# Turning and spilling the first batch's expert gates inside wavelet attention, and reading them back behind two experts' weights

## The reference

```python
logits = xt @ wg                                  # 128 channels -> 8 experts
topv, topi = jax.lax.top_k(logits, top_k)         # top_k = 2
w = jax.nn.softmax(topv, axis=-1)
gates = (jax.nn.one_hot(topi, E, dtype=x.dtype) * w[..., None]).sum(axis=1)
y = jnp.zeros_like(xt)
for e in range(E):                                # E = 8, hidden width 512
    h = jax.nn.gelu(xt @ w1[e] + b1[e])
    y = y + gates[:, e:e + 1] * (h @ w2[e] + b2[e])
```

## Time and profile before

| | us |
|---|---|
| median of 3 runs | 4427.36 |
| lowest and highest | 4424.29, 4433.59 |
| the profiled execution | 4442.52 |
| its span in the trace | 4441.2 |

### The profile page before, as it was taken

One profiled execution on the slowest core, in us unless ns is written; L12 is line 12 of the kernel. 1 busy time (PEld: TensorE's weight loads), 2 busy tenths in 40 slices (PEclk: granted clock), 3 DMA queues, 4 the chain that ended last, 5 costly groups with the idle time before them and its releaser, 6 DMA issues.

```text
span 4441.2 us, 73631 instructions
## 1 busy us (share of the span) xinstructions
PE 3571.8 (80%) x28566; PEld 1826.3 (41%) x28566; DVE 3318.2 (75%) x5155; ACT 2848.1 (64%) x4792; POOL 970.4 (22%) x1447
## 2 busy tenths in 40 slices
PE   6999868999799998999996555555555558899998
PEld 4666512222344445676673111111111115566666
DVE  6777767786311127887886999999999996778887
ACT  3655415556234445666665999999998995566665
POOL 2444432100467640000001222222221210000000
PEclk8999859999899999999997555555555559999999
DMA  1000031231412100000001101111101110000000
GB/s 48 1 1 1 1 72 32 55 57 20 108 28 38 38 17 9 12 7 12 2 2 22 22 15 22 22 22 22 21 16 22 22 19 20 7 11 7 7 2 21
DMA packets 256809, 97.45 MB, mean 22 GB/s; under 512 B 223795, under 2 KB 241854, under 8 KB 256446
## 3 DMA queue, kind: packets, MB, share of 16 engines
q1 hardware_dynamic: 256462, 92.74, 10.5%
HBM read 31.75 MB, written 2.23 MB: 8 GB/s over the span
## 4 chain that ended last, share of the span: by engine, by line
PE 43%; DVE 27%; issue 14%; ACT 3%; DMA 1%; SPq 0%; POOL 0%; DVEq 0%; POOLq 0%; ACTq 0%
DVE d_negmax L2802 12%; PE psum L2333 7%; PE psum L2362 6%; DVE f_m_E L2432 6%; PE psum L2348 6%; PE psum L2029 5%; PE psum L2052 5%; PE psum L1420 3%; DVE wl_negmax L1538 2%; PE psum L1409 2%; DVE f_pT_E L2451 2%; PE psum L1397 2%; ACT d_junk L2860 2%; PE psum L2735 1%; PE psum L2724 1%
## 5 line engine op out<-in xcount | busy, mean ns | idle before, releaser
L2802 DVE TENSOR_REDUCE d_negmax<-psum 128x1 f32<-128x1024 f32 x1024 | 1176.0, 1212 | 52.2 <-PE psum L2735 51.1
L2860 ACT ACTIVATE d_junk<-psum,d_negmax 128x1024 bf16<-128x1024 f32 x1024 | 1138.9, 1114 | 103.8 <-DVE d_negmax L2802 96.1
L2735 PE MATMUL psum<-d_qT,d_kT 64*128 64x512 bf16 x2048 | 607.1, 602 | 547.7 <-ACT d_junk L2860 527.1
L2526 ACT ACTIVATE hidden<-psum,f_nm_E 128x1024 f32<-128x1024 f32 x512 | 566.5, 1113 | 146.8 <-DVE f_nm_E L2435 146.7
L2432 DVE TENSOR_REDUCE f_m_E<-psum 128x1 f32<-128x1024 f32 x512 | 602.0, 1217 | 48.4 <-PE psum L2333 47.2
L2735 PEld LDWEIGHTS psum<-d_qT,d_kT 64*128 64x128 bf16 x2048 | 105.8, 101 | 1050.4 <-ACT d_junk L2860 990.0
L2333 PE MATMUL psum<-f_k_E,f_q_swapped_E 64*128 64x512 f32 x1024 | 526.3, 624 | 6.6 <-ACT hidden L2526 6.6
L2333 PE MATMUL psum<-f_k_E,f_q_E 64*128 64x512 f32 x1024 | 526.0, 623 | 2.9 <-DVE f_v_E L2423 1.9
L2362 PE MATMUL psum<-f_pT_E,f_v_E 128*64 128x128 f32 x8192 | 505.4, 276 | 2.5 <-DVE residual L2462 2.5
L2533 ACT COPY f_pT_E<-psum 128x512 f32<-128x512 f32 x512 | 299.9, 586 | 318.8 <-PE psum L2348 318.8
L2451 DVE COPY f_pT_E<-psum 128x512 f32<-128x512 f32 x512 | 351.5, 686 | 162.7 <-PE psum L2348 153.2
(11 more groups left out here) (330 smaller groups left out, 4542.8 us busy)
## 6 DMA issues: line engine op xcount, KB each, us to landing
moe_gates_on_all<-moe_gate_spill SPq DMA_DIRECT2D x16, 1024.0 KB, 13.7
f_q_swapped_E<-f_q_E SPq DMA_DIRECT2D x64, 128.0 KB, 2.3
moe_w<-in_moe_w SPq DMA_DIRECT2D x15, 256.0 KB, 5.6
out<-residual SPq DMA_DIRECT2D x1, 2048.0 KB, 8.7
residual<-in_hidden_states SPq DMA_DIRECT2D x2, 768.0 KB, 8.3
wl_qT<-wl_q_rows SPq DMA_TRANSPOSE x48, 3.3
residual<-in_hidden_states SPq DMA_DIRECT2D x2, 256.0 KB, 3.2
m_taps<-in_m_conv SPq DMA_DIRECT2D x4, 128.0 KB
```

The costliest lines, as they stand in the source:

```text
L2526: A.activation(pb[:, u % 2, f * 2 * BANK:(f + 1) * 2 * BANK], two(2 * f), ACT.Exp, bias=nm[:, u % 4:u % 4 + 1], scale=SC, accum_out=rs[:, ...
L2735: last = T.matmul(bank(2 + 2 * (at % 3) + jj), kT[half, s, jb * P:(jb + 1) * P], qT[half, s, hf * BANK:(hf + 1) * BANK], start=True, stop= ...
L2802: V.tensor_reduce(mh[:, t % 2, n // 2, n % 2:n % 2 + 1], two(2 + 2 * (at % 3)), X, ALU.max, negate=True).then_inc(*maxed.up(at))
L2860: A.activation(junk[:, at % 3, :], two(2 + 2 * (at % 3)), ACT.Exp, bias=mh[:, t % 2, n // 2, n % 2:n % 2 + 1], accum_out=sh[:, t % 2, n // ...
```

## The change

The first batch's transposition, copy and spill leave the head of phase D and become a step `dgt` in phase C's list, after unit 29 of the last round. It takes a slot of PSUM in the rotation. SP, which had no step left in phase C by then, issues the spill there. In phase D the reads of batch 0's gates (`moe_gates_8` and both halves of `gall`) go ahead of the weights of experts 2 to 7, behind those of experts 0 and 1. For batch 1 nothing moves. The list `late` loses its first entry, so the two banks swap parts.

```diff
+            def pe_gates(b, bk):
+                T.wait_ge(*fd.gated(b))
+                T.transpose(bank(bk)[:, 0:P], fd.gcol[:, :, :].rearrange("p e i -> p (e i)"), ident[:, :]).then_inc(*fd.g_turned.up(b))
+            def dve_rows(b, bk):
+                V.wait_ge(*fd.g_turned(b))
+                if b:
+                    V.wait_ge(fd.spilled.sem, 16 * b)
+                V.tensor_copy(fd.grow[:, :], bank(bk)[:, 0:P]).then_inc(*fd.g_copied.up(b))
+            def sp_rows(b):
+                SP.wait_ge(*fd.g_copied(b))
+                SP.dma_start(fd.spill[b].rearrange("e (i p) -> (e i) p", p=P), fd.grow[:, :]).then_inc(*fd.spilled.one())
...
-                                  25: [("dgate", 5), ("dgate", 6)], 26: [("dgate", 7)], 27: [("dgate", 8)]},
+                                  25: [("dgate", 5), ("dgate", 6)], 26: [("dgate", 7)], 27: [("dgate", 8)], 29: [("dgt",)]},
...
-                paired = [s for s in seq if s[0] in ("turn", "qkv", "max", "exp", "norm", "co", "wo", "yt", "dch", "dlg")]
+                paired = [s for s in seq if s[0] in ("turn", "qkv", "max", "exp", "norm", "co", "wo", "yt", "dch", "dlg", "dgt")]
...
+                        elif kind == "dgt":
+                            fd.sp_rows(0)
...
-                late = [("gt", 0)]
+                late = []
...
+                def sp_gates(k):
+                    b, g = groups[k]
+                    if g == 0:
+                        if b:
+                            fd.sp_rows(b)
+                        SP.wait_ge(*spilled.all())
+                        SP.dma_start(g8[:, b, :], spill[b]).then_inc(*few.one())
+                    if k >= 2:
+                        SP.wait_ge(*scaled((k - 1) * E_ - 1, FT - 1))
+                    for half in range(2):
+                        es = slice(half * E_ // 2, (half + 1) * E_ // 2)
+                        SP.dma_start(gall[:, k % 2, es], wide(spill[b:b + 1, es, g * BANK:(g + 1) * BANK], 0, P)).then_inc(*spread[k % 2][half].one())
...
                         SP.dma_start(w2[:, e * FT:(e + 1) * FT, :], a["moe_w2"][e].rearrange("(f p) d -> p f d", p=P)).then_inc(*ldw[e].one())
-                    for k, (b, g) in enumerate(groups):
-                        if g == 0:
-                            SP.wait_ge(*g_copied(b))
-                            SP.dma_start(spill[b].rearrange("e (i p) -> (e i) p", p=P), grow[:, :]).then_inc(*spilled.one())
-                            SP.wait_ge(*spilled.all())
-                            SP.dma_start(g8[:, b, :], spill[b]).then_inc(*few.one())
...
+                        if e == 1:
+                            sp_gates(0)
+                    for k in range(1, NGR):
+                        sp_gates(k)
...
                 def pe():
                     enter(T)
-                    pe_gates(0)
...
                 def dve():
                     enter(V)
-                    dve_rows(0)
```

More of the change, by code:

```diff
@@ L1096, in front_D @@
             mx = sb(st, "moe_max", [P, NT])
+            fd.grow = sb(st, "moe_gate_rows", [P, P])
+            fd.spill = nc.dram_tensor("moe_gate_spill", (NB, E_, S), F32).ap()
+            fd.spilled = loads("moe_gates_spilled")
+            fd.g_copied = signal("moe_gate_rows_done", range(NB))
             fd.ld = loads("moe_first_loads")
@@ L1160, in dve_gates @@
                 yield
-            fd.sp_first, fd.pe_logits, fd.act_gates, fd.dve_gates = sp_first, pe_logits, act_gates, dve_gates
+            fd.sp_first, fd.sp_rows, fd.pe_logits, fd.pe_gates = sp_first, sp_rows, pe_logits, pe_gates
+            fd.act_gates, fd.dve_gates, fd.dve_rows = act_gates, dve_gates, dve_rows
             return fd
@@ L1354, in pe_slot @@
                             T.wait_ge(*fd.lg_read(0))
+                        elif kind == "dgt":
+                            T.wait_ge(*fd.g_copied(0))
                         elif kind == "co":
@@ L1481, in pe @@
                             fd.pe_logits(0, pe_slot("dlg"))
+                        elif kind == "dgt":
+                            fd.pe_gates(0, pe_slot("dgt"))
                     leave(T)
@@ L1654, in dve @@
                             next(gates, None)
+                        elif kind == "dgt":
+                            fd.dve_rows(0, slot("dgt"))
                     leave(V)
@@ L1896, in phase_D @@
             GE = NG4 * E_
-            gated, g_turned, b1 = fd.gated, fd.g_turned, fd.b1
+            gated, g_turned, g_copied, b1, spill, spilled = fd.gated, fd.g_turned, fd.g_copied, fd.b1, fd.spill, fd.spilled
             fr = front_E("E", fd.stack)
@@ L1903, in phase_D @@
                 b2 = sb(st, "moe_b2", [E_, D])
-                grow = sb(st, "moe_gate_rows", [P, P])
                 gall = sb(st, "moe_gates_on_all", [P, 2, E_, BANK])
@@ L1910, in phase_D @@
                 yT = sb(st, "moe_yT", [P, 2, BANK])
-                spill = nc.dram_tensor("moe_gate_spill", (NB, E_, S), F32).ap()
                 ld, ldw = loads("phase_loads"), [loads(f"moe_expert_loads_{e}") for e in range(E_)]
-                spilled = loads("moe_gates_spilled")
                 again = loads("token_loads")
@@ L1927, in phase_D @@
                 added = signal("moe_added", range(NGR))
-                g_copied = signal("moe_gate_rows_done", range(NB))
                 FIRST_CH, AT_LG, AT_GT = 12, 16, 25
@@ L2005, in pe_route @@
                         yield
-                    pe_gates(b)
+                    fd.pe_gates(b, pe_late("gt", b))
                     yield
-                def pe_gates(b):
-                    T.wait_ge(*gated(b))
-                    T.transpose(bank(pe_late("gt", b))[:, 0:P], fd.gcol[:, :, :].rearrange("p e i -> p (e i)"), ident[:, :]).then_inc(*g_turned.up(b))
                 def pe_down(n):
@@ L2076, in dve_route @@
                     yield
-                    dve_rows(b)
+                    fd.dve_rows(b, late_bank("gt", b))
                     yield
[L2080 to L2084, removed]
                 def dve_copy(k):
```

## The result

| | before | after |
|---|---|---|
| median of 17 runs each, side by side, us | 4434.24 | 4425.09 |
| lowest and highest | 4424.29, 4442.08 | 4413.79, 4433.75 |
| ratio, 95% interval | | 0.9980 (0.9972 to 0.9988) |
| span of the profiled execution | 4441.2 | 4429.7 |

The change makes the kernel faster by 0.20%, 8.9 us (5 to 12). A second comparison, in another group of runs (12 of the changed kernel), gave 0.9989 (0.9978 to 1.0001), which alone does not tell the change from none. The forecast was 11.9 us and 4415.5 us. The direction and the place are right.

The account below looks back on a forecast made before the run. Transfers, no engine, bound phase D's head, then PE. Unit 2 starting at 1157.6 instead of 1169.51 saves 11.9 us, phase C costs 0: median 4427.4 becomes 4415.5 us; range 4408 to 4424, with rivals 4406 to 4428.

Parts of the forecast that it names:

- The bound and the anchor: Phase D's head waits for transfers; gain is how far unit 2's start moves from 1169.51, minus costs elsewhere.
- The turning in phase C: Transpose after unit 29 costs 0.17 to 0.33 us, phase D saves 0.17; together 0, bounds -0.2 and +1.2.
- The first half's landing: At phase D's head, first gate half lands at 1150.0 (1148.5 to 1152.4); POOL starts at 1150.25.
- Unit 0's second product: On PE at phase D's head: takes 4.6 to 5.8 us, freeing PE for unit 2 at 1156.3 to 1157.4.
- Expert 2's weights: At phase D's head, behind 2 MB of gates, they land at 1157.6, setting unit 2's start, 11.9 us earlier.
- waits for several microseconds: Sign of being wrong: unit 2 waits that long for moe_w; the forecast had under 1.5 us.
- SP held up: Rival: expert 2's loads stall behind the gate halves at phase D's head, about 4428 us; wholly or partly, chance 0.09.
- The clock: Rival: half-clock stretches in E and E2 take back 5 to 12 us, chance 0.11; make it slower, 0.05.
- I take the 11.9 off the median: Whole-kernel time: 11.9 us gain subtracted from the earlier runs' median of 4427.4, giving 4415.5 us.

Follow-up runs that it names:

- the second execution of this kernel: The changed kernel run and profiled once more with nothing altered; ratio to the kernel before 0.9989 (0.9978 to 1.0001), head 21.48 us.
- gates first: Changed kernel, with the gates' reads issued ahead of expert 1's weights too; ran once, 4430.74 us, head 29.62 us.
- weights between: Changed kernel, with expert 2's weights put between the two halves of the gates; ratio to the kernel before 0.9964, head 19.03 us.
- the order alone: Kernel before, with batch 0's spill and gate reads issued after expert 1's weights, all still in phase D; ratio 0.9973, head 23.37 us.
- the removed round trip alone: Kernel before, with only batch 0's turning, copy and spill moved into phase C, gate reads behind all weights; ratio 0.9991, head 27.61 us.

## Why the prediction was right or wrong

- **The bound and the anchor: right.** The waits at the head were transfers, and PE kept what it was spared: 450.4 us of phase D before, 450.5 after. Neither an engine nor a later phase took the gain back in any trace.
- **The turning in phase C: right.** The transpose stands on the path. From PE's release to the last value products it took 1113.51 - 1109.04 = 4.47 us, before 1113.62 - 1109.41 = 4.21: +0.26, between my 0.17 and 0.33. In phase D 0.17 went away (22.02 us from the last large copy to PE's first product, before 22.19). Together +0.1. The slot that came one place nearer cost nothing.
- **The first half's landing: right.** POOL started at 1149.67; I had 1150.25. Unit 0's second product took 4.70, I had 4.6 to 5.8.
- **Expert 2's weights: the term of the gain that was mis-sized.** I had worked out 1158.1 by the rates and 1157.7 by the landings and took 1157.6, below both; it was 1158.40. About 0.4 of these 0.8 us can be accounted for: from 1144 to 1154 the gates moved at a mean of 161 GB/s in place of my 167, by the one stretch at 117 (108 in the second execution of this kernel); why it was slower, and the rest of the 0.8, stay open. The wait that I had under 1.5 us was 2.62, and the head shrank by 10.7 (10.1 in the second execution), not by 11.9. Besides the 0.8, two small things make up that 1.2: the anchor was read off the chain (1169.51), 0.16 above the timeline, and phase D began 0.29 sooner, where the head does not count it. The first of the steps named to be *wrong* ("waits for several microseconds") was thus half true. Of the causes, order is shown (gates first, weights between), and SP's issue is excluded (both loads were out by 1142.75).
- **SP held up: wrong as a mechanism here.** SP did stand for 1.4 to 4.4 us in single loads, and 19.2 us in the tiny one after the residual, but all of that came after expert 2's loads had gone out, and no later unit of phase D waited for a transfer.
- **The clock: seen, at the wrong place.** I looked for it in phases E and E2, and took phase D's as 1.00 throughout; it costs 1.7 us at one place there, before and after the change alike. Behind phase D all twelve executions lie within 2817.9 to 2821.5 us. What varies is phase M's end and phase C's first round: 12 us between two executions of one kernel.
- **The absolute time: the failed step is "I take the 11.9 off the median".** The base was the median of 3 runs, 4427.36, out of a spread that its own three values, 9 us apart, showed. With 17 runs it was 4434.24, and in the other groups 4436.08 (23 runs) and 4430.88 (19). So 6.9 of the 9.6 us by which the forecast missed were in the base, and 2.7 in the gain (9.15 between the medians), of which the traces show 1.2. Either error alone would have left the time below the 4424 that the prediction gave for its forecast (4427.36 - 9.15 = 4418.2, 4434.24 - 11.9 = 4422.3); together they made 4425.09. The 15 us between the profiled execution and the median, which I had noted as scatter, had pointed there. The scatter of runs before around their median, which the range took as 4 to 6 us, was 3.1 and 6.2 in those three values and up to 10 us in the 17.
- **What stays open.** The ratios say 4.9 and 8.9 us, the heads 10.1 and 10.7. For the kernels with the order alone and with the weights between, the ratios say more than the heads (12.0 against 8.2, 16.0 against 12.5). The heads lie inside the 95% intervals of the ratios, except for the second comparison, whose interval ends at 9.7 us against 10.1. For the order alone 1.6 us of the difference are the clock in the rest of D, which the head leaves out. So the scatter of up to 12 us ahead of the change is enough for most of these differences; that the change does a little harm ahead of phase D is not excluded by them, but no trace shows it.

## What to carry to other kernels

Where a phase's head waits for transfers, write down the queue in order with each piece's bytes over the rate that its own kind shows, and look at what each consumer needs next: by the head the order alone was worth 8.2 us, the removed round trip alone 4.0, both together 10.7, and one more swap of two pieces another 1.9. Data read by all partitions from one row should be asked for before it is on the path, or copied in an idle stretch. And when a change is worth 0.2%, compare the stage that it touches between two landmarks in the trace: the head repeated within 0.6 us, where the time of single executions scattered by 20.

## What the runs showed of the hardware

- A read of the same DRAM row by all 128 partitions moved at 164 to 180 GB/s (117 in one stretch); the same bytes in the same 2 KB pieces from 128 rows moved at 376 to 395 GB/s.
- Transfers issued on one queue did not pass each other: unit 1, which waits for two 256 KB loads, started 13.3 us later with 2 MB ahead of them.
- The spill of 64 KB, 5.93 us behind weights, landed in 1.6 us on an idle queue.
- Two executions of the same program were granted 0.75 and 0.91 of TensorE's clock over the same 80 us, and were 12 us apart when phase D began.
